# State-space loop of a two-layer decoder: for seven of the sixteen states GpSimd multiplies the drive of the second channel half, from rows of B broadcast through DRAM

## The reference

```python
xz = x @ W_in.T
xc, z = jnp.split(xz, 2, axis=-1)            # 256 channels each
xc = silu(causal_conv(xc, W_conv))
dbc = xc @ W_xproj.T                         # 8 + 16 + 16 columns
dlt, Bm, Cm = dbc[..., :8], dbc[..., 8:24], dbc[..., 24:]
delta = softplus(dlt @ W_dt.T + b_dt)
A = -jnp.exp(A_log)
deltaA  = jnp.exp(delta[..., None] * A)
deltaBx = delta[..., None] * Bm[:, :, None, :] * xc[..., None]
def step(h, inp):
    dA, dBx, c = inp
    h = dA * h + dBx
    return (h, jnp.einsum('bdn,bn->bd', h, c))
y = scan(step)(deltaA, deltaBx, Cm) + xc * D
y = y * silu(z)
return y @ W_out.T
```

## Time and profile before

| | us |
|---|---|
| median of 3 runs (2075.86 to 2083.24) | 2076.91 |
| the profiled execution | 2077.34 |
| its span, first to last instruction | 2075.6 |
| TensorE busy in the span | 1959.6 (94%) |
| VectorE busy | 1570.3 (76%) |
| ScalarE busy | 1356.3 (65%) |
| GpSimd busy | 98.5 (5%) |

### The profile page before, as it was taken

The page is one execution under the profiler, slowest core; times in us unless marked ns, Lnnn a source line. Parts: engine busy times, 40 slices in busy tenths (PEclk is TensorE's granted clock), DMA queues, the critical chain, the costliest instruction groups (busy, mean ns, idle before and its releaser), DMA issues. The chain is left out here.

```text
span 2075.6 us, 38309 instructions
## 1 busy us (share of the span) xinstructions
PE 1959.6 (94%) x15036; PEld 1024.4 (49%) x15036; DVE 1570.3 (76%) x3006; ACT 1356.3 (65%) x2401; POOL 98.5 (5%) x84
## 2 busy tenths in 40 slices
PE   7778999999999999999999998998999989999897
PEld 2224744444444444444444444675344445777755
DVE  7997899999999999999999942233888854444344
ACT  5334488888888888888888886333588853333421
POOL 1661000000000000000000000002000000000000
PEclk9999999999999999999999999999999998999999
DMA  4210000000000000000000000110000000000011
GB/s 145 71 61 0 1 1 2 2 1 2 2 1 2 2 2 1 2 2 1 2 2 2 1 1 1 37 38 13 1 1 1 1 1 1 1 1 0 13 31 28
DMA packets 22853, 24.73 MB, mean 12 GB/s; under 512 B 5712, under 2 KB 20080, under 8 KB 22432
## 3 DMA queue, kind: packets, MB, share of 16 engines
q1 hardware_dynamic: 21504, 20.37, 3.2%
q10 hardware_dynamic: 1184, 2.10, 0.3%
HBM read 21.74 MB, written 0.59 MB: 11 GB/s over the span
## 5 line engine op out<-in xcount | busy, mean ns | idle before, releaser
L986 DVE TENSOR_REDUCE sb_max_partial<-ps_max_ps 128x1 f32<-128x512 f32 (+1 forms) x1664 | 977.1, 660 | 44.1 <-PE ps_max_ps L796 43.2
L970 ACT ACTIVATE sb_probs<-ps_score_ps 128x512 f32<-128x512 f32 (+1 forms) x1632 | 873.9, 597 | 110.9 <-PE ps_score_ps L934 65.8
L934 PE MATMUL ps_score_ps<-sb_q_stack,sb_key_stack 64*128 64x512 f32 x1632 | 586.7, 444 | 3.9 <-ACT sb_probs L970 3.4
L796 PE MATMUL ps_max_ps<-sb_key_stack,sb_q_stack 64*128 64x512 f32 (+1 forms) x1560 | 556.0, 438 | 0.0
L923 PE MATMUL ps_acc_ps<-sb_probs,sb_val_ones 128*32 128x256 f32 x6528 | 465.1, 387 | 0.2 <-ACT sb_probs L970 0.2
L934 PEld LDWEIGHTS ps_score_ps<-sb_q_stack,sb_key_stack 64*128 64x128 f32 x1632 | 277.1, 184 | 326.1 <-ACT sb_probs L970 267.0
L796 PEld LDWEIGHTS ps_max_ps<-sb_key_stack,sb_q_stack 64*128 64x128 f32 x1560 | 265.2, 184 | 9.6 <-DVE sb_max_partial L986 7.4
L923 PEld LDWEIGHTS ps_acc_ps<-sb_probs,sb_val_ones 128*32 128x32 f32 x6528 | 156.5, 109 | 207.0 <-issue 142.8
L1639 DVE TENSOR_REDUCE sb_s_max_partial<-ps_s_ps 128x1 f32<-128x512 f32 x256 | 158.5, 680 | 24.4 <-PE ps_s_ps L1548 24.1
L1626 ACT ACTIVATE sb_s_probs<-ps_s_ps 128x512 f32<-128x512 f32 x256 | 140.5, 597 | 26.7 <-PE ps_s_ps L1576 19.1
L1922 DVE TENSOR_SCALAR_CACHE_REDUCE sb_x_scores<-ps_x_score_ps 128x1024 f32<-128x1024 f32 (+1 forms) x56 | 62.1, 1110 | 83.3 <-PE ps_x_score_ps L1863 83.3
(11 more groups left out here) (267 smaller groups left out, 1825.3 us busy)
## 6 DMA issues: line engine op xcount, KB each, us to landing
sb_val<-c_rows SPq DMA_DIRECT2D x16, 512.0 KB, 3.7
sb_e_w<-L_ffn_rW SPq DMA_DIRECT2D x30, 128.0 KB, 2.1
sb_e_w<-L_ffn_W_T SPq DMA_DIRECT2D x24, 128.0 KB, 2.1
sb_ctx_T<-ctx_T SPq DMA_DIRECT2D x1, 1664.0 KB, 7.5
sb_ctx_T<-ctx_T ACTq DMA_DIRECT2D x1, 1538.0 KB, 8.8
sb_x_T<-x_T SPq DMA_DIRECT2D x1, 512.0 KB, 3.7
sb_x_tok<-x ACTq DMA_DIRECT2D x1, 512.0 KB, 11.4
sb_e_w<-L_ffn_sW SPq DMA_DIRECT2D x4, 128.0 KB, 2.4
```

The source lines that it names most:

```text
L796: nc.tensor.matmul(bank((blk, u))[:, 0:n], queries, keys, start=True, stop=True).then_inc(tile_ready, 1)
L934: nc.tensor.matmul(score_ps[:, e % 3, :], k.key_stack[rows(blk), c * P:(c + 1) * P], q_stack[rows(blk), blk // 2, j * HALF:(j + 1) * HALF] ...
L970: nc.scalar.activation(probs[0:n, c % 3, j * HALF:(j + 1) * HALF], score_ps[0:n, e % 3, :], ACT.Exp).then_inc(exp_done, 1)
L986: nc.vector.tensor_reduce(partial[:, blk % 2, h, r:r + 1], bank((blk, u))[:, 0:RANGES[r][1]], AX.X, ALU.max).then_inc(tile_used, 1)
```

## The change

For the states in `POOLED`, which are 2, 4, 6, 8, 10, 12 and 14, the drive of the second half (`s == 1`) is no longer made by TensorE and VectorE.

- GpSimd multiplies `u[1]` with row `n` of B, both in SBUF, into the SBUF tile `pool_drive`. It does so for state `n+1` directly behind its read of `(n, 0)`.
- The row comes from DRAM: the tensor that held C's 16 rows now holds B's 16 and C's 16 (`bc_rows`), and SyncE broadcasts a row of B into one of two buffers `b_wide`, seven times in all, between its loads of C. The first two wait for `b_rows_moved` and `dlt_ready`, since their places held `dbc`; the later ones wait for an earlier `pool_driven`.
- TensorE leaves out those seven spreads, and VectorE those seven drives. Their scans take `pool_drive` instead of `drive[1]`, and wait for `pool_driven`.

```diff
@@ mamba, names
-        c_dram = nc.dram_tensor("c_rows", (NS, T), F32, kind="Internal").ap()
+        bc_dram = nc.dram_tensor("bc_rows", (2 * NS, T), F32, kind="Internal").ap()
+
+        POOLED = list(range(2, NS - 1, 2))
+        b_wide = [k.key1_T[:, 4 * T:5 * T], early[:, 5 * T:6 * T]]
+        pool_drive = k.key1_T[:, 5 * T:6 * T]
...
+        def load_b(sp, i):
+            if i >= 2:
+                sp.wait_ge(pool_driven, i - 1)
+            else:
+                sp.wait_ge(dlt_ready, 2)
+                sp.wait_ge(b_moved, 16 * 2 * GROUPS)
+            if i > 0:
+                sp.wait_ge(b_loaded, 16 * i)
+            n = POOLED[i]
+            sp.dma_start(b_wide[i % 2], bc_dram[n:n + 1, :].to_broadcast([P, T])).then_inc(b_loaded, 16)
@@ SyncE
-                sp.dma_start(c_dram, dbc[DR + NS:ROWS, :]).then_inc(c_stored, 16)
+                sp.dma_start(bc_dram, dbc[DR:ROWS, :]).then_inc(c_stored, 16)
...
                     load_c(sp, n)
+                    if n + 1 in POOLED:
+                        load_b(sp, POOLED.index(n + 1))
@@ GpSimd
                         nc.gpsimd.tensor_tensor(read[:, s, :], state[:, s, :], c_all[:, n % DEPTH, :], ALU.mult).then_inc(read_ready, 1)
+                        if pooled(n + 1, 1 - s) and s == 0:
+                            i = POOLED.index(n + 1)
+                            pool.wait_ge(b_loaded, 16 * (i + 1))
+                            if i > 0:
+                                pool.wait_ge(scanned, 2 * POOLED[i - 1] + 2)
+                            nc.gpsimd.tensor_tensor(pool_drive, u[:, 1, :], b_wide[i % 2], ALU.mult).then_inc(pool_driven, 1)
@@ TensorE
-                            spread(pe, n + 1, s)
+                            if not pooled(n + 1, s):
+                                spread(pe, n + 1, s)
@@ VectorE
-                        dve.wait_ge(b_ready, 2 * n + s + 1)
-                        nc.vector.tensor_tensor(drive[s], drive[s], u[:, s, :], ALU.mult).then_inc(driven, 1)
-                        dve.wait_ge(driven, 2 * n + s + 1)
+                        if pooled(n, s):
+                            dve.wait_ge(pool_driven, POOLED.index(n) + 1)
+                        else:
+                            dve.wait_ge(b_ready, drives_to(n, s))
+                            nc.vector.tensor_tensor(drive[s], drive[s], u[:, s, :], ALU.mult).then_inc(driven, 1)
+                            dve.wait_ge(driven, drives_to(n, s))
...
-                        nc.vector.tensor_tensor_scan(state[:, s, :], decay[:, s, :], drive[s], 0.0, ALU.mult, ALU.add).then_inc(scanned, 1)
+                        nc.vector.tensor_tensor_scan(state[:, s, :], decay[:, s, :], pool_drive if pooled(n, s) else drive[s], 0.0, ALU.mult, ALU.add).then_inc(scanned, 1)
```

9 lines of the change are left out of this document (7 added, 2 removed).

## The result

| | before | after |
|---|---|---|
| median, us | 2079.26 (2075.86 to 2083.24, 5 runs) | 2092.69 (2086.60 to 2097.26, 5 runs) |
| the profiled execution, us | 2077.34 | 2092.83 |
| its span, us | 2075.6 | 2090.9 |
| mean granted clock of TensorE | 0.975 | 0.962 |

The change makes the kernel slower: the ratio is 1.0069, 95% interval 1.005 to 1.0087.

The account below looks back on a forecast made before the run. The prediction took VectorE to bound the loop, which is serial with all later stages. It added +9.1 (seven pairs), +2.1 (a half-clock pair) and -0.7 (the old wait) to 2077.3, giving 2087.8, rounded to 2088 us; range 2076 to 2100.

Parts of the forecast that it names:

- What bounds the kernel: In the loop, VectorE works 112.7 of 115.2 us and sets its length; the loop is serial with later stages.
- the ceiling of 8.7 us: Seven drives of 1.25 us leave VectorE: at most 8.7 us saved, 0.42%, if nothing else becomes late.
- GpSimd's chain of three: Read (n, 0), multiplication, read (n, 1) back to back on GpSimd, ending 7.15 us after scan (n, 0), delaying the pooled scan.
- The pair without interference: Two states, n odd and n+1 even, without VectorE and GpSimd excluding each other: 13.4 us instead of 13.8.
- The exclusion holds for a scan: A pooled scan with two SBUF inputs and a GpSimd read wait for each other; no exclusion had chance 0.12.
- Who comes first: At the pooled scan, GpSimd's read (n+1, 0) gets the port before VectorE: +1.3 us a pair, +9.1 for seven.
- The clock: TensorE's clock drops to half behind gaps between adds; one such pair more than today, about +2.1 us.
- The old slow pair: Half-clock stretch at the loop's start, partly relieved as a 0.74 us wait for a removed spread goes: -0.7 us.
- Edits at no cost: Larger DRAM store, seven broadcasts of B and ScalarE's decays stay covered; if a cover failed, up to 3.7 us once.
- VectorE gets the port first: Rival: pooled scan before GpSimd's read, +0.3 us a pair; 2079, or 2083 with some half clock; chance 0.2.
- the clock falls again and again: Rival: TensorE's gap in every pair halves the clock repeatedly; four pairs 2094, all seven 2100; chance 0.28.

Follow-up runs that it names:

- e13_all_fills: Changed kernel with pooled decay in PSUM, GpSimd's multiplication before read (n, 0), and zero matmuls in state 0 and before odd-n adds (n, 0); 2070.63 us, ratio 0.9963.
- e14_before_fill0: Kernel before the change, with matmuls of zeros on TensorE in state 0 only; 2079.30 us against 2078.19, ratio 1.0003.
- e2_psum: Changed kernel, but ScalarE writes the pooled halves' decay into PSUM, so the pooled scan has one SBUF input; 2077.97 us against 2077.99 before, ratio 0.9998.
- e3_unused: Kernel before plus the change's broadcasts of B and GpSimd multiplications, results unused, all spreads and drives kept; 2079.54 us against 2077.99, ratio 1.0006.
- e5_psum_fill: Changed kernel with pooled decay in PSUM and two matmuls of zeros replacing each left-out spread; 2077.52 us against 2078.52 before, ratio 0.9992.
- e11_fill_both: Changed kernel with two matmuls of zeros replacing each left-out spread and two before the add of (n, 0), n even; 2085.02 us against 2078.52 before, ratio 1.0034.
- e9_psum_early: Changed kernel with pooled decay in PSUM and GpSimd's multiplication ahead of its read of (n, 0); 2073.22 us against 2078.52 before, ratio 0.9973.

## Why the prediction was right or wrong

The forecast was 2088 us, the range 2076 to 2100; 2092.7 was measured. Slower by over 0.5% had the chance 0.47 and is what came (0.69%); the prediction had given slightly more, 0.51, to a change within 0.5%.

- **What bounds the kernel, and the ceiling of 8.7 us:** right. e13_all_fills against e14_before_fill0 gives 8.5 in the loop.
- **GpSimd's chain of three:** right in kind, ending 7.1 behind scan (n, 0) instead of 7.15. Two GpSimd instructions do not leave 0.06 us between them but overlap by 0.04 (70.99, 73.31 and 75.62 are 2.32 and 2.31 apart, with rows of 2.36 and 2.35). The pair without interference was to take 13.4, and did in e2_psum.
- **The exclusion holds for a scan:** right. The row of line 663, 3.25 us instead of 1.22, carried over to another operation. Both values worked out for it were seen: 14.1 with VectorE first, 15.0 with GpSimd first (predicted 14.1 and 15.1). The rule of the Trainium skill (SBUF — State Buffer, Who interferes with whom), that whoever issues first holds the port to its end, fits here, though the page says it of VectorE's two-port modes: reads of 4.05 to 4.35 us where VectorE was first, scans of 4.32 to 4.36 where GpSimd was, and neither when the scan has an input in PSUM.
- **Who comes first:** wrong. I put the end of scan (n+1, 0) at 6.9 and of read (n, 1) at 7.15. The 6.9 took a VectorE without waits; but drive (n, 1) waited 0.32 for its spread (71.18), so the scan ended at 7.3, and VectorE was first in all seven pairs. I had said that the margin was a few hundredths; what I had missed is that the order of one pair decides that of the next. Taken alone this error made the forecast 6.9 us too high (9.1 instead of 2.2).
- **The clock:** the term that was far too small. I took one pair at half clock, at +2.1; five pairs were slow, at +2.3 to +3.2 over a pair of 14.09, 14.0 in all. The count was the main error: one pair, where five came. I argued that the adds around the gap would hold the clock, and saw only one gap of 2.7 us; the held read makes a second (2.39 and 1.92 us in the full-clock pair), and once the clock is down a gap of 3.4 comes. The 17 us named for a slow pair did appear, but as 14.1 + 3.2, not as 15.1 + 2.1.
- **The old slow pair:** I gave 0.7 back. It went from 15.3 to 14.09; counting 0.3 for the exclusion, 1.5 came back. The reason that I gave, the spread that is gone, is not the one: e3_unused makes that spread and has the same 14.09, and e5_psum_fill, which leaves it out, has 15.2. How low the clock is in the first pair varies from trace to trace.
- **Edits at no cost:** right as far as can be told; e3_unused has them all and no slower pair, and its median is 1.55 us above that of before, with no change inside the interval.

By its own terms the sum should have read 7 x 0.3 = +2.2 for the exclusion with VectorE first, +14.0 for the clock and -1.5 for the old slow pair: +14.7, where it read +9.1, +2.1 and -0.7. The number was near by luck, because two errors had opposite signs: 6.9 us too much for the order, 11.9 too little for the clock. Of the rivals, "VectorE gets the port first" and "the clock falls again and again" came true together; I had priced the first with at most 4 us of clock (2079 to 2083) and the second on the wrong pair (2094).

What is shown and what is not: that the input in PSUM removes the loss is shown (e2_psum), that work in both gaps keeps the clock behind the first pair is shown (e11_fill_both), and that the gaps of the exclusion bring the clock down follows from the two together. The exclusion is not the only thing that does: e9_psum_early has none, and its clock fell in four pairs. Why one pair of 14.09 keeps its clock and the next one does not was not found.
